# Strassen's seven block products for the queries and keys of the second attention layer

## The reference

```python
def _L1_attn_ref(hidden_states, wq, wkv, wo):        # H=32 heads, DN=128, DR=64, DV=128, HID=512
    q = jnp.einsum('bsd,de->bse', hidden_states, wq).reshape(B, S, H, DQ)
    kv = jnp.einsum('bsd,de->bse', hidden_states, wkv)
    k = kv[..., :H * DN].reshape(B, S, H, DN)
    v = kv[..., H * DN:H * (DN + DV)].reshape(B, S, H, DV)
    scale = DQ ** (-0.5)
    scores = jnp.einsum('bqhd,bkhd->bhqk', q[..., :DN], k) * scale
    causal = jnp.tril(jnp.ones((S, S), dtype=bool))
    scores = jnp.where(causal[None, None], scores, NEG_INF)
    probs = jax.nn.softmax(scores, axis=-1)
    attn = jnp.einsum('bhqk,bkhd->bqhd', probs, v).reshape(B, S, H * DV)
    return jnp.einsum('bse,ed->bsd', attn, wo)
```

## Time and profile before

| | us |
|---|---|
| median of 3 runs (range) | 1553.34 (1552.18 to 1555.84) |
| the profiled execution's own time | 1558.95 |
| its span | 1557.2 |
| PE busy in the span | 1494.2 (96%) |
| DVE busy | 1099.4 (71%) |
| ACT busy | 767.8 (49%) |
| POOL busy | 484.7 (31%) |
| DMA | 88.60 MB, mean 57 GB/s |

### The profile page before, as it was taken

The page is one execution under the profiler, slowest core; times in us unless marked ns, Lnnn a source line. Parts: engine busy times, 40 slices in busy tenths (PEclk is TensorE's granted clock), DMA queues, the critical chain, the costliest instruction groups (busy, mean ns, idle before and its releaser), DMA issues. The chain is left out here.

```text
span 1557.2 us, 29364 instructions
## 1 busy us (share of the span) xinstructions
PE 1494.2 (96%) x8993; PEld 1309.0 (84%) x8993; DVE 1099.4 (71%) x2790; ACT 767.8 (49%) x2153; POOL 484.7 (31%) x537
## 2 busy tenths in 40 slices
PE   6999999998689979999999999999999999999898
PEld 5889898897477868888888898888888988888786
DVE  3788888887577656666666767666666666666665
ACT  3787887786344524434344444443444443434421
POOL 3455555554231013213213312311321321330321
PEclk9999999999799999999999999999999999999999
DMA  4223323322344531011011011011101101100001
GB/s 161 62 72 82 78 72 84 76 73 61 97 130 139 139 122 54 2 55 54 0 54 54 0 54 54 21 33 54 48 6 54 54 0 54 54 0 13 1 14 41
DMA packets 47954, 88.60 MB, mean 57 GB/s; under 512 B 6064, under 2 KB 14768, under 8 KB 47920
## 3 DMA queue, kind: packets, MB, share of 16 engines
q1 hardware_dynamic: 47920, 88.16, 19.8%
HBM read 77.66 MB, written 2.10 MB: 51 GB/s over the span
## 5 line engine op out<-in xcount | busy, mean ns | idle before, releaser
L98 PE MATMUL c_bj<-g_xT_hi,b_w 128*128 128x512 f32 x512 | 214.8, 420 | 2.8 <-PEq L926 2.8
L99 PE MATMUL c_bj<-g_xT_lo,b_w 128*128 128x512 f32 x512 | 203.7, 398 | 0.0
L100 PE MATMUL c_bj<-g_xT_hi,b_w 128*128 128x512 f32 x512 | 203.3, 397 | 0.0
L462 POOL TENSOR_TENSOR h_pr<-h_pr,h_rinv 128x512 f32<-128x512 f32 x128 | 133.2, 1040 | 132.0 <-DVE h_rinv L553 129.6
L1144 POOL CAST b_w<-b_raw_q 128x512 fp32r<-128x512 f32 x32 | 20.5, 641 | 435.7 <-PE c_bj L100 435.7
L98 PE MATMUL c_bj<-b_w,g_xT_hi 128*128 128x256 f32 x512 | 143.5, 280 | 0.0
L99 PE MATMUL c_bj<-b_w,g_xT_hi 128*128 128x256 f32 x512 | 143.4, 280 | 0.0
L100 PE MATMUL c_bj<-b_w,g_xT_lo 128*128 128x256 f32 x512 | 142.9, 279 | 0.0
L492 ACT ACTIVATE h_pr<-h_bs,h_nmax 128x256 f32<-128x256 f32 x256 | 118.6, 473 | 6.6 <-DVE h_nmax L548 6.6
L1376 DVE TENSOR_TENSOR c_v_lo<-c_bj,c_v_hi 128x256 fp32r<-128x256 f32 x128 | 54.4, 425 | 93.9 <-ACT c_v_hi L1288 93.9
L1380 DVE TENSOR_TENSOR g_res<-c_bj,g_res 128x512 f32<-128x512 f32 x128 | 88.3, 692 | 45.4 <-PE c_bj L100 42.8
(11 more groups left out here) (265 smaller groups left out, 4643.6 us busy)
## 6 DMA issues: line engine op xcount, KB each, us to landing
f_wi<-in_w_ffn SPq DMA_DIRECT2D x66, 256.0 KB, 2.7
h_part<-in_w_ffn SPq DMA_DIRECT2D x32, 264.0 KB, 2.8
h_o_mix<-h_o_hi SPq DMA_DIRECT2D x64, 128.0 KB, 2.2
b_raw_q<-in_w_attn SPq DMA_DIRECT2D x32, 256.0 KB, 6.5
b_raw_k<-in_w_attn SPq DMA_DIRECT2D x32, 256.0 KB, 7.2
b_raw_v<-in_w_attn SPq DMA_DIRECT2D x16, 512.0 KB, 7.4
b_raw_o<-in_w_attn SPq DMA_DIRECT2D x16, 512.0 KB, 3.9
a_w<-in_w_head SPq DMA_DIRECT2D x32, 225.0 KB, 2.6
```

What stands on the lines that cost most here:

```text
L98: pe.matmul(out, w[0], x[0], start=start, stop=False, skip_group_check=True)
L99: pe.matmul(out, w[0], x[1], start=False, stop=False, skip_group_check=True)
L100: return pe.matmul(out, w[1], x[0], start=False, stop=stop, skip_group_check=True)
L462: pool.tensor_tensor(pr[b][:, :, :], pr[b][:, :, :], rinv[b][:, :][:, :, None].to_broadcast([P, 2, S]), ALU.mult)\
```

## The change

Queries and keys of one head for all tokens are taken as a product of 2 x 2 blocks: the 512 hidden numbers in halves, the tokens in halves, and queries and keys as the two kinds of result. Strassen's scheme in Winograd's form makes it from seven products of blocks instead of eight. Each block product is 6 matmuls of 128x512 (two chunks of 128 hidden numbers, three matmuls each).

- The work goes head by head: a unit is one head, four steps, one for each batch `t`.
- POOL makes the four sums of weight blocks (`combine`: four TENSOR_TENSOR of 128x256 in the tile `slots`), then four splits into `sw` (one of 256 and three of 512 columns), and the lo parts of three of the four results (`rest`, 128x512 each). It still splits values (even heads) and outputs (odd heads), 1024 columns each.
- Four token sums (`ts`) are made once in the prologue, by DVE, ACT and POOL. Two sums that they need are made by POOL at the end of FFN0 (`first_blocks`).
- p1, p6, p7, p4 of a head add up in one bank, `bx`, and ACT copies the bank to the scratch `y` between them. p2, then p5 and p3 go to bank `by`, and DVE adds them to `y` (`total`); ACT makes hi (`sum_hi`), POOL makes lo (`rest`). The first half of the keys comes straight from `bx` (`key_hi`, `key_lo`).
- Even heads (`hd` 0) carry the eight output tiles of the group before, odd heads the value tiles of the group after, two a step. All of them go to one bank, `bv`.
- SP loads a head's query and key weights (two transfers of 256 KB) into `slots`, which has one buffer, after the last split of the head before.
- FFN1's weights are loaded behind the last product; their splits come one step later.

```diff
                 after.power(pool, 0)
+                attn1.first_blocks(pool, after)
...
+    GROUPS = ((0, 1), (1, 3), (3, 5), (5, 7))
...
+    def load_qk(self, sp, h):
+
+        need(sp, self.s_wlo, 4 * h)
+        w = self.io["w_qk1"][bass.ds(h, 1), :, :, :].rearrange("a p i n -> (a p) i n")
+        slots = self.slots[:, :].rearrange("p (i n) -> p i n", n=self.BLOCK)
+        sp.dma_start(slots[:, 0:4:2, :], w[:, 0:2, :]).then_inc(self.s_in["qk"], 16)
+        sp.dma_start(slots[:, 5:8:2, :], w[:, 2:4, :]).then_inc(self.s_in["qk"], 16)
...
+        pool.wait_ge(self.s_in["qk"], 32 * h + 32)
+        need(pool, self.s_wlo, 4 * h)
+        put(self.S1, self.A21, self.A22, ALU.add)
+        put(self.S3, self.A11, self.A21, ALU.subtract)
+        pool.wait_ge(self.s_comb, 4 * h + 1)
+        put(self.S2, self.S1, self.A11, ALU.subtract)
+        pool.wait_ge(self.s_comb, 4 * h + 3)
+        put(self.S4, self.A12, self.S2, ALU.subtract)
+        pool.wait_ge(self.s_comb, 4 * h + 4)
...
-                with sp.Fori(1, NG) as gr:
-                    self.load(sp, gr)
...
+                    if has(2 * gr + 3, NH):
+                        self.load_qk(sp, 2 * gr + 3)
+                    if has(gr + 2, NG):
+                        self.load(sp, "v", gr + 2)
+                    if has(2 * gr + 4, NH):
+                        self.load_qk(sp, 2 * gr + 4)
+                    if has(gr + 1, NG):
+                        self.load(sp, "o", gr + 1)
...
-                    if has(gr + 1, NG):
-                        self.split(pool, "q0", gr + 1, [(s_jmm[0], r + 1)])
-                        self.split(pool, "k0", gr + 1, [(s_jmm[0], r + 2)])
-                        self.split(pool, "v", gr + 1, [(s_jmm[2], r + 2)])
-                        self.split(pool, "q1", gr + 1, [(s_jmm[0], r + 3)])
-                        self.split(pool, "k1", gr + 1, [(s_jmm[0], r + 4)])
-
-                    self.split(pool, "o", gr, [(s_jmm[2], r + 4)])
...
+                        self.combine(pool, h + 2)
+                        self.split_qk(pool, h + 2, 0, [(s_x, 4 * h + 5)])
+                    if now:
+                        rest(h + 1, 0, q0)
+                    if hd == 0 and has(gr + 1, NG):
+                        self.split(pool, "v", gr + 1, [(s_vmm, 4 * gr + 4)])
+                    if hd == 1 and has(gr, NG):
+                        self.split(pool, "o", gr, [(s_omm, 8 * gr)])
+                    if more:
+                        self.split_qk(pool, h + 2, 1, [(s_x, 4 * h + 6), (s_y, 3 * h + 4)])
+                    if now:
+                        rest(h + 1, 1, k1)
+                    if more:
+                        self.split_qk(pool, h + 2, 2, [(s_x, 4 * h + 7), (s_y, 3 * h + 5)])
+                    if now:
+                        rest(h + 1, 2, q1)
+                    if more:
+                        self.split_qk(pool, h + 2, 3, [(s_x, 4 * h + 8), (s_y, 3 * h + 6)])
+
...
+                def copy(h, i):
+
+                    act.wait_ge(s_x, 4 * h + i + 1)
+                    need(act, s_sumlo, 3 * (h - 1) + (1, 3, 2)[i])
+                    act.activation(y[:, i, :], bx[:, :], ACT.Identity, scale=(SCALE1, SCALE1, 1.0)[i])\
+                       .then_inc(s_copy, 1)
+
+                def sum_hi(h, par, i):
+                    act.wait_ge(s_sum, 3 * h + i + 1)
+                    kind, half = ((0, 0), (1, 1), (0, 1))[i]
+                    act.activation(qk[par][:, 0, kind, half * HALF:(half + 1) * HALF], y[:, (0, 2, 1)[i], :],
+                                   ACT.Identity).then_inc(s_sumhi, 1)
+
+                def key_hi(h, par):
+                    act.wait_ge(s_x, 4 * h + 4)
+                    act.activation(qk[par][:, 0, 1, 0:HALF], bx[:, :], ACT.Identity).then_inc(s_khi, 1)
...
+                def total(h, i):
+
+                    n = (0, 2, 1)[i]
+                    dve.wait_ge(s_y, 3 * h + i + 1)
+                    dve.wait_ge(s_copy, 3 * h + n + 1)
+                    if i == 1:
+                        m = dve.tensor_tensor(y[:, n, :], by[:, :], y[:, n, :], ALU.add)
+                    else:
+                        m = dve.scalar_tensor_tensor(out=y[:, n, :], in0=by[:, :], scalar=SCALE1, in1=y[:, n, :],
+                                                     op0=ALU.mult, op1=ALU.add)
+                    m.then_inc(s_sum, 1)
...
+                        if hd == 0 and t == 0 and not (isinstance(gr, int) and gr == 0):
+                            value_lo(4 * gr + 3, 3)
+                        if has(s + 1, NSTEP):
+                            softmax_a(s + 1, (t + 1) % 4)
+                        if has(s - 1, NSTEP):
+                            outs(s - 1, hd if t else 1 - hd, (t - 1) % 4)
+                        if has(s, NSTEP):
+                            probs(s)
+                        if has(s + 1, NSTEP):
+                            softmax_b(s + 1, (t + 1) % 4)
+                        if t == 2 and has(h + 1, NH):
+                            key_lo(h + 1, 1 - hd)
+                        if hd == 0 and has(gr - 1, NG):
+                            add_out(8 * (gr - 1) + 2 * t, 2 * t, bv)
+                        if t < 3 and has(h + 1, NH):
+                            total(h + 1, t)
+                        if hd == 0 and has(gr - 1, NG):
+                            add_out(8 * (gr - 1) + 2 * t + 1, 2 * t + 1, bv)
...
-                    if kind == "qk":
-                        n = QK[t]
-                        pe.wait_ge(s_wlo[n], gr + 1)
-                        tok = slice(c * HALF, (c + 1) * HALF)
-                        for kc in range(KC):
-                            w = tuple(x[:, kc * P:(kc + 1) * P] for x in ws[n])
-                            m = matmul3(pe, bj[0][:, :], w, (xhi[:, kc, tok], xlo[:, kc, tok]), kc == 0, kc == KC - 1)
...
-                    for bank in range(3):
-                        if todo.get(bank) == "o":
-                            if t == 2 and bank == 1:
-                                pe.wait_ge(s_olo, s - 2)
-                        project(todo, bank, r, *unit, t)
...
+                def product(h, i, slot, x, bank, start, done):
+
+                    pe.wait_ge(s_wlo, 4 * h + i + 1)
+                    n = self.BLOCK
+                    for c in range(2):
+                        a = slot * n + c * P
+                        w = tuple(z[:, a:a + P] for z in self.sw)
+                        m = matmul3(pe, bank[:, :], w, tuple(z[:, c, :] for z in x), start and c == 0, c == 1)
+                    m.then_inc(done, 1)
...
+                def p1(h):
+                    need(pe, s_klo, h)
+                    product(h, 0, self.A11, tokens(0, 0), bx, True, s_x)
+
+                def p6(h):
+                    pe.wait_ge(s_copy, 3 * h + 1)
+                    product(h, 1, self.S2, self.ts[1], bx, False, s_x)
...
+                def p2(h):
+                    need(pe, s_sum, 3 * h)
+                    product(h, 1, self.A12, tokens(1, 0), by, True, s_y)
...
+                        def tile(i):
+                            if hd == 0 and has(gr - 1, NG):
+                                if t + i == 0:
+                                    pe.wait_ge(s_vlo, 4 * gr + 4)
+                                else:
+                                    pe.wait_ge(s_oadd, 8 * (gr - 1) + 2 * t + i)
+                                out(gr - 1, 2 * t + i, bv)
+                            if hd == 1 and has(gr + 1, NG):
+                                if t + i == 0:
+                                    need(pe, s_oadd, 8 * gr)
+                                if i == 0:
+                                    pe.wait_ge(s_vlo, 4 * gr + 4 + t)
...
+                        if t < 3:
+                            if has(h + 1, NH):
+                                (p6, p7, p4)[t](h + 1)
+                            tile(0)
+                            if has(h + 1, NH):
+                                (p2, p5, p3)[t](h + 1)
+                            tile(1)
+                        else:
+                            tile(0)
+                            if has(h + 2, NH):
+                                p1(h + 2)
+                            tile(1)
+                        pe.wait_ge(s_vlo, 4 * gr + t + 1)
+                        values(s, hd, t)
...
+                    p1(0)
+                    both_tiles(0)
+                    p2(0)
+                    both_tiles(1)
+                    for j in late:
+                        before.turn(pe, j, turned)
+                    pe.wait_ge(*before.split_until(NT - 3))
+                    both_tiles(2)
+                    pe.wait_ge(*before.split_until(NT - 1))
+                    both_tiles(3)
+                    pe.wait_ge(s_tslo, 1)
...
+                    pe.wait_ge(s_tslo, 1)
+                    p6(0)
+                    pe.wait_ge(s_tslo, 2)
+                    p5(0)
+                    pe.wait_ge(s_tslo, 3)
+                    p7(0)
```

(98 more changed lines are left out.)

558 lines of the change are left out of this document (287 added, 271 removed).

## The result

The changed kernel takes 1570.66 us (median of 4 runs, 1568.84 to 1573.65) against 1554.59 (1552.18 to 1556.25): ratio 1.0107, 95% interval 1.0084 to 1.0129, 16 us slower. The forecast was 1559, the range 1531 to 1600: the way was right, and a third of the size.

What follows compares the result with a forecast made beforehand. PE was taken as the bound. −44.6 (matmuls) + 31.6 (waits) + 6 (contention) + 7.5 (prologue) + 1 (end) + 1 (FFN0) + 3 (POOL's cycle) = +5.5, giving 1559 us against 1553.34; range 1531 to 1600.

Steps and rivals of the forecast that it cites:

- A: Odd heads, t = 3: PE waits 0.88 us ahead of the first value tile until DVE's lo part frees the bank.
- B: Even heads, t = 3: PE waits 0.74 us ahead of the second output tile for DVE's addition of the first.
- C: Even heads, t = 0: DVE's lo part of the last value tiles delays its addition, PE waits 0.19 us.
- Removed matmuls: Queries and keys on PE: 1344 matmuls instead of 1536, 192 x 0.232 = −44.6 us, 2.8 a group.
- POOL beside DVE: POOL's subtractions hold DVE's two softmax normalizations, ahead of additions PE waits for: 0 to +17, taken +6 us.
- The prologue: Token sums and products ahead of the first turn make it 12.6 us later: +7 lost, plus 0.5 for shorter first steps.
- The end: FFN1's first matmul waits for the layer norm behind the last outputs: 0 to +2, taken +1 us.
- FFN0's 1: Late in FFN0, POOL's two `first_blocks` operations may hold DVE's splits: 0 to +2.4, taken +1 us.
- POOL's own cycle: POOL's work per head takes 26 to 31.5 us against PE's 27.9: 0 to +99, taken +3 us.
- rival 1: POOL becomes the bound with a cycle of 29 or 30 us a head: 1580 to 1610 us; chance 0.30.
- rivals 2 and 3: 2: waits A and B half as long, about 1534 to 1542, chance 0.13; 3: only the prologue lost, 1518, chance 0.08.
- Rival 4: Nothing saved: contention holds the softmax in most steps, C grows to 0.8 for three t, +38, 1591 us; chance 0.06.

Runs made afterwards that it cites:

- the holds: POOL's splits in even heads held behind DVE's softmax of steps 0 and 1, against the changed kernel: 1565.97 us; steps 0 to 2, with both orders changed: 1537.00 us.
- A alone: Against the changed kernel, PE takes product p1 ahead of the first value tile in the last step of odd heads: 1557.93 us.

## Why the prediction was right, and where it was off

The main argument held: the matmuls go, and waits for one bank eat them. The sum forecast +5.5 and +16 was measured, for the losses outside A, B and C were put too low. That 1570.7 lies in the stated range is little proof, as the range was 69 us wide.

1. *Removed matmuls, −44.6.* Right as far as the runs show it. A product of the same size put in again costs 29.2 us where it still covers the wait B and 37.3 where next to no wait is left, for 42 of matmuls.
2. *Waits A, B, C, +31.6.* Shown: A and B measured 0.85 and 0.71, and taken away they gave 12.7 and 14.2 us, 29.4 together; by the loop 0.82, 0.81 and 1.69 a group, where 0.96 and 0.81 were expected with the start. DVE's order in the step, not its speed, set them: B went with the same operations in another order.
3. *POOL beside DVE, +6.* The mechanism is right, the size somewhat small. L1461 averages 426 ns and L1462 446 from 700 to 1400, where 289 and 349 stood before. The collisions in steps 0 and 1 cost 0.14 and 0.35 on average and one more start, 0.6 us a group or 9 in all. This is read from the traces; no run took the collisions away, the holds only moved them.
4. *The prologue, +7.5.* The first turn was forecast 12.6 later and came 12.9 later (from the stage's start), which is partly luck, by parts that were off against each other: the token sums began earlier than I took, the four lo parts took 1.7 each and not 1.3, since POOL made weight sums beside them (6.75 us for 2.95). The term that failed is the 0.5 "for shorter first steps". From the stage's first matmul to step 4 it is 58.6 us before and 69.3 after, with 6 matmuls of 0.232 fewer: 12.1 lost. The value tiles that went into the prologue are missing in the first steps, which then last as long as the softmax's chain, not as long as their matmuls, and here POOL's subtractions held that chain. The last key part (L1505) stands behind the two normalizations, and PE's scores of step 3 wait for it (the row names POOL, which was done at 609.36; L1505 ends at 610.12):

```profile
608.15 1.36 DVE L1462 TENSOR_SCALAR c_pr<-c_pr,c_rinv 128x256 f32<-128x256 f32 x1
...
610.22 0.55 PE L1661 MATMUL c_bs<-c_qk 128*128 128x256 f32 x1 [2.82 <-POOL c_qk L1291]
```

L1461 ahead of it took 1.28 us. Behind this pause the granted clock stood at 0.50 (1.2 GHz) from 610 to 614 us. Both vary from one execution to the next: with A alone, which has the same prologue, PE stood only 1.5 us there, the clock was 1.00 from 608 to 616, and the first stretch took 66.5 us and not 69.3. So some 3 of the 12.1 belong to this execution. A rise "up to 10" for POOL and a lower clock was in the prediction's bounds.
5. *The end, +1, was too low.* From step 116 to FFN1 it took 76.7 us before and takes 79.3, with 18 matmuls (4.2 us) fewer: 6.8, of which a group's usual loss is 2.8 or 2.9. The other 3.9 were not separated. PE waited 1.4 in each of three steps for the last outputs' lo parts, 1.95 for the last even head's tile and 3.4 ahead of FFN1, where POOL still had its last splits; in the kernel before it stood 1.98, 1.78, 2.06 and 1.75 at other places of the same stretch. Both executions also had some us at a lower granted clock there (0.64 from 1460 to 1464 and 0.57 from 1476 to 1480 before, 0.72 and 0.50 from 1464 to 1472 after).

Put together: −44.6 + 15 x 2.8 + 12.1 + 3.9 = +13.4; the stage and what follows grew by 14.1. Against the forecast's +5.5 items 2 and 3 together add 4.4 (42.0 for 37.6), items 4 and 5 add 4.6 and 2.9, and POOL's 3 and FFN0's 1 fall away. What `first_blocks` did to FFN0 can't be told.

6. *POOL's own cycle, +3, rival 1.* Wrong in its working. I read the 0.81 of the earlier trace rows as time that POOL's loop costs ahead of every split. After the change splits follow without it:

```profile
1004.08 1.29 POOL L1291 TENSOR_TENSOR c_qk<-g_y,c_qk 128x512 fp32r<-128x512 f32 x1 [4.22 <-ACT c_qk L1375]
1005.31 0.61 POOL L1168 CAST b_sw_hi<-b_slots 128x512 fp32r<-128x512 f32 x1
...
1011.44 2.95 POOL L1150 TENSOR_TENSOR b_slots<-b_slots 128x256 f32<-128x256 f32 x4 [4.15 <-DMA b_slots<-in_w_qk]
```

In the kernel before, that split waited for a value tile, as ACT did, which started at the same moment (POOL's row is at 1046.87):

```profile
1046.75 0.38 ACT L1288 ACTIVATE c_v_hi<-c_bj 128x256 fp32r<-128x256 f32 x1 [1.01 <-PE c_bj L100]
```

The two transfers of weights landed in 3.0 us each, and POOL stood 4.2 ahead of the sums, the low end of the 4 to 7. POOL's work of a head and this wait are about 22 us of 28, and the rest it stands idle for PE and ACT; rival 1 never came near, and rivals 2 and 3 fall with the measured waits. Rival 4 named the contention, in a size that was too large: 0.6 us a group against 2.5. That nothing was left of the gain, as it said, came mostly from A and B.

Of the signs one missed: PE's busy time fell by 24.8 us (1494.2 to 1469.4), not by some 43, and groups took 56.5 us, not 55.5 to 56.

## What to carry to other kernels

Matmuls that stand between two uses of one bank are that bank's cover (here of B; A was covered by order alone, with no matmul added): before they are removed, count the time until the engine that empties the bank is done, by its place in that engine's order. Work taken from the full engine is won only if the order of the others is made anew with it; here two swapped blocks turned 1% slower into 1% faster. Not tried: two banks for the tiles, as the kernel before had; all eight are in use in the changed one, so another tile would have had to give one up. A gap marked "issue" is to be held against the start of other engines at the same moment before it is called overhead.

## What the runs showed of the hardware that I had not expected

Sums and differences with SBUF inputs on POOL are held by DVE as well as the other way round: four of 256 columns took 6.75 us beside DVE's four of 1024 columns and 2.95 alone, and DVE's took 6.78 beside them and 4.62 alone. The Trainium skill ("SBUF — State Buffer", "Who interferes with whom") has the later one blocked for the whole length of the other; the trace agrees, for the two alone add up to 2.95 + 4.62 = 7.6 and together took 7.8 (574.18 to 582.02 us), as if one after the other. Holding POOL back did not remove these collisions but moved them to the next softmax.
